# A causal mask moved from TensorE into VectorE's maxima, and k's rotation moved behind them, in an attention and expert layer

## The reference

```python
q, k, v = (proj(Wq), proj(Wk), proj(Wv))          # 16 heads of 32
q, k = _apply_rope(q, k)
scores = jnp.einsum('bhqd,bhkd->bhqk', q, k) / jnp.sqrt(HEAD_DIM)
scores = jnp.where(causal[None, None], scores, jnp.finfo(scores.dtype).min)
attn = jax.nn.softmax(scores, axis=-1)
out = jnp.einsum('bhqk,bhkd->bhqd', attn, v)      # then  out @ Wo.T
...
top_vals, top_idx = jax.lax.top_k(gate_logits, 2) # 8 experts, two for each token
y_all = jnp.einsum('td,eod->teo', xf, expert_w) + expert_b[None, :, :]
out = jnp.sum(y_sel * w[:, :, None], axis=1)      # w: softmax of the two logits
```

## Time and profile before

| | |
|---|---|
| median of 3 runs | 995.77 us (995.76 to 997.95) |
| the profiled execution's own time | 1002.43 us |
| its span, first to last instruction | 1000.6 us |
| mean granted clock of PE | 0.98 |
| busy PE / DVE / POOL / ACT | 93% / 75% / 56% / 44% |
| steps 17 to 27 | 21.05 us each |

### The profile page before, as it was taken

How to read it: one execution, slowest core, us unless ns; L and a number is a source line. 1 busy time by engine, 2 the same in 40 slices (tenths; PEclk the granted TensorE clock), 3 DMA queues, 4 the chain that set the end, 5 groups by cost and what they waited for, 6 DMA issues and landing times.

```text
span 1000.6 us, 18754 instructions
## 1 busy us (share of the span) xinstructions
PE 932.2 (93%) x6589; PEld 448.1 (45%) x6589; DVE 746.0 (75%) x1327; ACT 435.6 (44%) x711; POOL 555.9 (56%) x553
## 2 busy tenths in 40 slices
PE   2899888988999999989999999989999999999897
PEld 1344334444444444535555555534444444444333
DVE  7888987887889899944444444477788888788865
ACT  5267865855755443331112211224434444344432
POOL 1545575574575556662333333247877888777641
PEclk9999999998999999999999999999999999999989
DMA  6366588698587344395655555454555554555431
GB/s 239 106 222 214 158 277 303 181 305 300 175 264 291 123 159 138 142 313 167 201 175 175 178 169 176 158 205 149 187 175 180 178 191 139 162 186 179 142 107 54
DMA packets 107963, 188.63 MB, mean 189 GB/s; under 512 B 11872, under 2 KB 65248, under 8 KB 102624
## 3 DMA queue, kind: packets, MB, share of 16 engines
q1 hardware_dynamic: 97072, 152.03, 44.1%
q0 software_dynamic: 10800, 35.40, 12.4%
HBM read 117.13 MB, written 70.25 MB: 187 GB/s over the span
## 4 chain that ended last, share of the span: by engine, by line
PE 68%; DVE 12%; DMA 7%; POOL 6%; ACT 4%; issue 2%; SPq 1%; DVEq 0%; ACTq 0%; POOLq 0%
PE psum L947 18%; PE psum L1032 11%; PE psum L1056 6%; PE psum L995 6%; PE psum L982 6%; PE psum L1041 5%; PE psum L998 5%; PE psum L964 5%; DMA x_in<-x 4%; PE psum L924 3%; DVE top L1482 3%; PE psum L966 2%; POOL gT L579 1%; POOL k_hl L588 1%; DMA xT_rows<-gT 1%
## 5 line engine op out<-in xcount | busy, mean ns | idle before, releaser
L760 ACT ACTIVATE pT<-psum,factors 128x512 f32<-128x512 f32 (+1 forms) x352 | 219.6, 640 | 253.8 <-PE psum L982 234.0
L1482 DVE TENSOR_REDUCE top<-psum 128x1 f32<-128x384 f32 (+3 forms) x352 | 210.5, 634 | 23.4 <-PE psum L966 22.4
L1032 PE MATMUL psum<-xT,w_att 128*128 128x512 f16 x768 | 197.5, 383 | 6.9 <-DVE xT L1433 5.0
L947 PE MATMUL psum<-w_exp,x_gT 128*128 x852 | 197.0, 381 | 0.9 <-issue 0.9
L964 PE MATMUL psum<-k_stack,q_stack 96*128 96x384 f16 (+3 forms) x512 | 128.8, 305 | 19.6 <-DVE top L1482 18.8
L608 POOL DMA_INDIRECT x_g<-xn_rows,tok_of x71 | 67.5, 951 | 135.8 <-PE psum L924 134.3
L982 PE MATMUL psum<-q_stack,k_stack 98*128 98x256 f16 (+3 forms) x512 | 129.3, 305 | 6.0 <-ACT pT L760 4.7
L1438 DVE TENSOR_TENSOR x_gT<-psum,x_gT 128x512 f16<-128x512 f32 x71 | 49.1, 692 | 105.2 <-ACT x_gT L784 85.1
L947 PEld LDWEIGHTS psum<-w_exp,x_gT 128*128 128x128 f16 x852 | 83.7, 98 | 87.2 <-issue 3.4
L784 ACT ACTIVATE x_gT<-psum 128x512 f16<-128x512 f32 x71 | 42.5, 598 | 172.2 <-PE psum L924 170.2
L592 POOL TENSOR_SCALAR_AFFINE_SELECT pT<-pT 128x512 f32<-128x512 f32 x128 | 94.8, 751 | 20.4 <-ACT pT L760 20.4
(11 more groups left out here) (175 smaller groups left out, 1282.9 us busy)
## 6 DMA issues: line engine op xcount, KB each, us to landing
y_rows<-y_sb SPq DMA_DIRECT2D x71, 256.0 KB
w_in<-w_all SPq DMA_DIRECT2D x12, 1024.0 KB, 9.6
q_stack<-qk_rows SPq DMA_DIRECT2D x96, 128.0 KB
k_stack<-qk_rows SPq DMA_DIRECT2D x96, 128.0 KB
x_in<-x SPq DMA_DIRECT2D x8, 1024.0 KB, 13.3
qk_rows<-q_hl SPq DMA_DIRECT2D x32, 256.0 KB
qk_rows<-k_hl SPq DMA_DIRECT2D x32, 256.0 KB
xn_rows<-x_in SPq DMA_DIRECT2D x8, 1024.0 KB, 4.9
```

The lines of the kernel that those rows point to most:

```text
L760: act.activation(p_of(j, h, heads), banks[BANK_T + (NT_ * n + k) % 2][:, 0:W], ACT.Exp, scale=factors[:, 0:1]).then_inc(exp_done, 1)
L947: now = pe.matmul(banks[s % 4], x_gT[s % 4][:, xp * C + c, :], w_exp[:, bass.ds(e, 1), wp, c, :].rearrange("p e d -> p (e d)"), start=n == ...
L1032: now = pe.matmul(bank, w_att[:, what, wp, c, g * P:(g + 1) * P], xT[b % 2][:, xp * C + c, :], start=at_pass == 0, stop=at_pass == 3 * C - 1)
L1482: return dve.tensor_reduce(out=top[:, h:h + heads, i], in_=banks[BANK_S + k % 2][:, 0:heads * W].rearrange("p (h t) -> p h t", h=heads), a ...
```

## The change

For groups m of 17 to 31 and units of one head PE no longer adds the mask; DVE's maximum adds it from SBUF while it reduces, and writes the sums back into the bank. The mask tensor gets 384 columns of zeros in front, so that a slice that ends behind the first head's mask covers a unit of any width. In steps 16 to 28 DVE rotates k behind maximum 10 and `split_c` instead of between maxima 8 and 9, and POOL takes k's low half behind mask 3 instead of ahead of mask 2. `slot_f` is moved onto the memory of `rest`, to make room.

```diff
-    causal = at("causal", [P, HG, P], BF16)
+    keep_all = S - P
+    causal = at("causal", [P, keep_all + HG * P], BF16)
...
-    slot_f = at("slot_f", [P, 2, NT], F32)
...
+    slot_f = at("slot_f", [P, 2, NT], F32, slot[2])
...
+    def masked_there(m, k):
+        return m > N1 and S_UNITS[k][1] == 1
...
-            own.link(pool.affine_select(out=causal[:], in_=causal[:], compare_op=ALU.is_ge, fill=MASKED,
+            masks = causal[:, keep_all:keep_all + HG * P].rearrange("p (h t) -> p h t", h=HG)
+            own.link(pool.affine_select(out=masks, in_=masks, compare_op=ALU.is_ge, fill=MASKED,
                                         base=0, pattern=[[0, HG], [-1, P]], channel_multiplier=1))
...
@@ POOL, step(n) @@
-                if n + 3 < N:
+                if n < N1:
                     low_qk(1, n + 3)
...
                 mask(n, 3)
+                if n >= N1 and n + 3 < N:
+                    low_qk(1, n + 3)
...
@@ PE, scores(m, k) @@
+                there = masked_there(m, k)
                 for h in range(heads):
-                    pe.matmul(bank[:, h * W:(h + 1) * W], ..., start=h == 0, stop=False)
-                pe.matmul(..., ident16[:], causal[:, 0:heads, :], start=False, stop=True).then_inc(s_done, 1)
+                    now = pe.matmul(bank[:, h * W:(h + 1) * W], ..., start=h == 0, stop=there)
+                if not there:
+                    now = pe.matmul(..., ident16[:], causal[:, keep_all:keep_all + heads * P]..., start=False, stop=True)
+                now.then_inc(s_done, 1)
...
@@ DVE, largest_score(m, k) @@
-                return dve.tensor_reduce(out=top[:, h:h + heads, i], in_=banks[BANK_S + k % 2][:, 0:heads * W]...,
-                                         axis=AX.X, op=ALU.max).then_inc(max_done, 1)
+                of = banks[BANK_S + k % 2][:, 0:heads * W]
+                if masked_there(m, k):
+                    dve.tensor_tensor_reduce(of, of, causal[:, keep_all + P - W:keep_all + P], 1.0, MASKED, ALU.add, ALU.max, top[:, h, i:i + 1])\
+                        .then_inc(max_done, 1)
+                else:
+                    dve.tensor_reduce(out=top[:, h:h + heads, i], in_=of..., axis=AX.X, op=ALU.max).then_inc(max_done, 1)
...
@@ DVE, step(n) @@
-                if ahead:
+                if n < N1:
                     rotate(1, n + 3)
...
                     largest_score(n + 1, 10)
                     split_c(n + 1)
+
+                if n >= N1 and ahead:
+                    rotate(1, n + 3)
```

More of the change, by code:

```diff
@@ L962, in scores @@
                     pe.wait_ge(c_copied, m)
+                there = masked_there(m, k)
                 for h in range(heads):
[L964 to L967, removed]
+                    now = pe.matmul(bank[:, h * W:(h + 1) * W], q_stack[u][0:ROW_C, h0 + h, i * P:(i + 1) * P], k_stack[u][0:ROW_C, h0 + h, 0:W],
+                                    start=h == 0, stop=there)
+                if not there:
+                    now = pe.matmul(bank[:, 0:heads * W].rearrange("p (h t) -> p h t", h=heads)[:, :, W - P:W], ident16[:],
+                                    causal[:, keep_all:keep_all + heads * P].rearrange("p (h t) -> p h t", h=heads), start=False, stop=True)
+                now.then_inc(s_done, 1)
             def turn_c(m):
@@ L1481, in largest_score @@
                 dve.wait_ge(s_done, NS * m + k + 1)
-                return dve.tensor_reduce(out=top[:, h:h + heads, i], in_=banks[BANK_S + k % 2][:, 0:heads * W].rearrange("p (h t) -> p h t", h=heads),
-                                         axis=AX.X, op=ALU.max).then_inc(max_done, 1)
+                of = banks[BANK_S + k % 2][:, 0:heads * W]
[3 more added lines that the diff above has]
+                else:
+                    dve.tensor_reduce(out=top[:, h:h + heads, i], in_=of.rearrange("p (h t) -> p h t", h=heads), axis=AX.X, op=ALU.max)\
+                        .then_inc(max_done, 1)
             def split_c(m):
```

## The result

The changed kernel took 1008.93 us (median of 4 runs, 1007.32 to 1010.71), the kernel before 996.55 beside it: a ratio of 1.0143, 95% interval 1.0116 to 1.0169. It is slower by 12.4 us; 12.8 had been forecast.

What follows compares the result with a forecast made beforehand. PE was taken as full in steps 17 to 27, with DVE and POOL close behind. The terms 12.1 + 1.5 - 0.8 = +12.8 us on 995.77 gave 1008.6 us; range 994 to 1026, likeliest case 1006 to 1014.

Steps and rivals of the forecast that it cites:

- Where the loss lies: Steps 17 to 27: k's late rotation delays POOL's mask 1, PE waits ahead of times_v(n, 1); +1.1 us a step, chance 0.60.
- The masks: PE's dropped mask matmuls: units 4 to 7 give nothing, unit 3 0.06 us, units 8 and 9 0.12, unit 10 0.06.
- The masks win nothing net by this point: At score unit 10's start: unit 8 starts 0.15 us later, 0.12 is won back, so 820.97 against 820.94.
- The maximum: DVE's maximum that adds the mask: one instruction of 749 ns, 0.07 us dearer each, between bounds of 0 and 0.23.
- 0.23 dearer: Upper bound for DVE's new maximum as two instructions, 749 and 164 ns, 913 together; the whole would then be 1013 us.
- two prices for POOL's block: Rope k and mask 1 beside DVE's expert adds: 4.43 us from step 16, or 4.7 by step 23's own prices.
- +1.5: Step 28: late rotation delays mask 1 to 934.1 against times_v at 932.24; 0.3 to 0.4 of the 1.9 comes back.
- -0.8: Steps 29 and 30 rotate nothing; mask matmuls of units 6 to 10 are won, -0.4 us each step.
- Other edits: Low k behind mask 3 fits POOL's wait of 1.90 us and leaves no second wait at mask 2; the others cost nothing.
- The clock: Rival, slower still: PE's stall drops the granted clock to 0.50 in eleven steps, 17.6 us more, 1026 us; chance 0.10.
- The lock does not bind: Rival, no change: split_c runs at once behind maximum 10, mask 1 ends just in time at 828.0; 996 to 998 us, chance 0.13.
- The masks come out whole: Rival, faster: k's path fits its slack, PE's chain shrinks by 8 x 0.06 us a step; 988.6 us, chance 0.17.

## Why the prediction was right

**Where the loss lies: right.** It named the path unit 10, `split_c` held by low q, rotation, rope k beside the adds, mask 1, times_v(n, 1). Each piece came out: the first of `split_c` until low q's end, the third free (0.17 for 1.14), 4.43 us for POOL's block, 8.07 us from unit 10 to times_v(n, 1) against 8.08 to 8.33 forecast. That this is the cause, and not only where the time shows, is shown by three runs: the rotation alone makes the loss, and taking away either half of it (the order, the adds' length) takes it all away.

**The masks: right.** "The masks win nothing net by this point": legs one and two of the table, and 0.9995 for the masks alone. That the masks of units 4 to 6 are worthless because DVE sets unit 8 is shown by the version that leaves them on PE and gains 0.26 us a step, where 0.22 was expected; with them on DVE too the gain is 0.06.

**The maximum: right in size, short in form.** The trace shows two instructions (groups of the window of nearly ten steps):

```profile
L1496 DVE CUSTOM_DVE_ANT_0 psum<-psum,causal 128x512 f32<-128x512 f32 x40 | 27.8, 718 | 4.9 <-PE psum L974 4.9
...
L1496 DVE CUSTOM_DVE_ANT_0 psum<-psum,causal 128x384 f32<-128x384 f32 x40 | 21.9, 567 | 0.0
...
L1496 DVE DVE_READ_ACCUMULATOR2_ANT top<- 128x1 f32 x80 | 11.5, 143 | 0.0
```

I had taken one of 749. The Trainium skill's rule (VectorE: DVE Perf Modes, "Two Vector instructions with no wait between them"), that an accumulator written out makes two, holds here. But the sum that I had worked out by it, 0.23 dearer, does not: the read begins before the first ends (824.72 against 824.10 + 0.70), so the result stands 0.76 after the start at 512 columns against 0.68 before, 0.08 more.

**Sizes.** A step was +0.97, forecast +1.1: I had taken the middle of two prices for POOL's block, and the lower, from step 16, was exact. Step 16 up to times_v(16, 1) took 7.72 in both, forecast 0. From there to times_v(27, 1), eleven steps, it was 231.57 and is 242.18: 10.6 for 12.1. From there to times_v(28, 2) it was 25.24 and is 26.77: +1.5, as forecast.

From times_v(28, 2) to PE's last wait it was 57.96 and is 57.12, -0.84 where -0.8 was forecast, but this agreement is in part luck, since the granted clock (third figure from the end) differs. Before, changed, rotation alone:

```profile
937.48:995.44 57.96, 52.55 (x428) 22.53 (x429) 36.66 (x71) 22.35 (x38) 21.41 (x28) 0.91 0.31 94
```

```profile
946.59:1003.71 57.12, 51.05 (x413) 20.69 (x414) 37.81 (x88) 22.07 (x38) 21.42 (x28) 0.94 0.31 95
```

```profile
946.05:1000.77 54.72, 48.84 (x430) 21.12 (x428) 36.76 (x72) 21.99 (x38) 22.02 (x27) 1.00 0.32 98
```

The rotation alone saves no mask there and is still, at a clock of 1.00, 3.2 us shorter than before. At the clock of before, 0.91, the versions with short adds and with masks where no score unit waits took 57.60 and 57.46, 0.36 and 0.50 less than before. So I put the masks of steps 29 and 30 at about 0.4 in all, half of the forecast, and the rest of the 0.84 down to the clock.

The sum by the trace is 11.3; the medians say 12.4, whose interval begins at 11.6. The rest is in no instruction that I could find; one profile of each kernel cannot tell it from what such falls of the clock move.

**Other edits: right, for a reason that held in one step.** Low k behind mask 3 takes its 1.16 out from ahead of mask 2. With it back, ten of eleven steps are as long, so there no second wait was there to save. In the one with a late gather it was (0.91).

**The rivals.** The clock stayed at 1.00 through all the steps with their idle 0.95 us. "The lock does not bind" failed at `split_c`'s first row, 0.76 for 0.16; the version that takes the rotation past the lock has, at 995.66, about the time that this rival gave (996 to 998). "The masks come out whole" failed without the rotation too, in the masks alone.

## What to carry to other kernels

On a full engine, price a saved instruction only up to the next point where that engine already waits; here four of the eight saved matmuls stood ahead of such a point, and leaving three of these on PE turned nothing into a gain of 3.7 us (by the medians). When an instruction moves within one queue, ask of each new neighbour whether it shares something with another engine: here a rotation that reads PSUM passed by a busy GpSimd, a 16-column operation with both inputs in SBUF did not (0.76 us for 0.16), and their order was worth some 13 us. Slack on a path has to be counted with what will run beside it then, not with what runs beside it now.

## What was not expected of the hardware

Idle times of PE of the same length, in step 28, had different ends. In the changed kernel the granted clock stayed at 1.00 behind it; with the rotation alone, and with low k back, it went to 0.50 (rows of PE, then busy time by stretch, for each kernel):

```profile
941.82 0.85 PE L1007 MATMUL psum<-pT,v_sb 128*32 128x384 f32 x8 [2.07 <-POOL pT L599]
```

```profile
941.80:944.00 2.20, 2.18 (x20) 0.82 (x21) 0.51 (x1) 0.74 (x2) 1.62 (x3) 1.00 0.04 11
```

```profile
939.68 1.51 PE L1007 MATMUL psum<-pT,v_sb 128*32 128x384 f32 x8 [2.08 <-POOL pT L599]
```

```profile
939.60:942.00 2.40, 2.32 (x16) 0.60 (x16) 0.57 (x1) 0.80 (x2) 1.82 (x4) 0.50 0.01 3
```

```profile
939.59 1.50 PE L1005 MATMUL psum<-pT,v_sb 128*32 128x384 f32 x8 [2.08 <-POOL pT L599]
```

```profile
939.60:942.00 2.40, 2.40 (x16) 0.58 (x16) 0.47 (x1) 0.71 (x2) 1.82 (x3) 0.50 0.04 10
```

So the length of one idle time does not tell whether the clock falls, as my rival had assumed from the earlier trace rows; what else decides was not tried.
